# Reordering the start-up loads and PE's fillers, and splitting the last unit into half pairs, in a two-layer conditional convolution kernel

## What is computed

```python
# layer 0
x = x + conv1d(x, weight, groups=4, padding=4) + (cond @ c_weight.T)[:, :, None] + fside[None, :, None]
# layer 1
h = gelu(cond @ W0 + b0); h = gelu(h @ W1 + b1)
att = softmax(h @ W2 + b2)                      # (128, 8)
agg_w = einsum('bk,koi->boi', att, weight)      # one 64x64 matrix a sample
agg_b = att @ bias_k
x = x + einsum('boi,bih->boh', agg_w, x) + agg_b[:, :, None]
```

## Time and profile before

| | us |
|---|---|
| median of 3 runs (lowest, highest) | 248.84 (248.31, 249.13) |
| the profiled execution | 249.11 |
| its span in the trace | 247.3 |
| PE busy | 237.3 (96%) |
| DVE busy | 220.3 (89%) |
| ACT busy | 126.6 (51%) |
| POOL busy | 10.4 (4%) |

### The profile page before, as it was taken

The page is one execution under the profiler, slowest core; times in us unless marked ns, Lnnn a source line. Parts: engine busy times, 40 slices in busy tenths (PEclk is TensorE's granted clock), DMA queues, the critical chain, the costliest instruction groups (busy, mean ns, idle before and its releaser), DMA issues.

```text
span 247.3 us, 5763 instructions
## 1 busy us (share of the span) xinstructions
PE 237.3 (96%) x2162; PEld 103.9 (42%) x2162; DVE 220.3 (89%) x113; ACT 126.6 (51%) x208; POOL 10.4 (4%) x36
## 2 busy tenths in 40 slices
PE   6799999999999999999999999999999999999991
PEld 4643334344344444444444444444444444444530
DVE  1075899999999999999999999999999999999582
ACT  2457007374535456383645445373745446263772
POOL 1325000000000000000000000000000000000000
PEclk9689999999999999999999999999999999999999
DMA  7998566999999999999999999999999997444448
GB/s 189 307 326 240 152 125 191 258 312 365 357 322 268 359 263 383 249 380 238 334 294 292 327 256 378 247 388 239 362 273 322 298 281 293 170 170 172 171 184 328
DMA packets 28555, 68.39 MB, mean 277 GB/s; under 512 B 3184, under 2 KB 3568, under 8 KB 28544
## 3 DMA queue, kind: packets, MB, share of 16 engines
q1 hardware_dynamic: 19104, 50.98, 62.3%
q10 hardware_dynamic: 9440, 17.26, 26.5%
HBM read 34.67 MB, written 33.55 MB: 276 GB/s over the span
## 4 chain that ended last, share of the span: by engine, by line
PE 91%; DVE 3%; ACTq 2%; ACT 1%; issue 1%; DVEq 0%
PE yps L528 64%; PE zps L551 21%; PE yps L608 3%; DVE ynat L433 2%; ACTq L285 2%; PE yps L565 1%; PE zps L577 1%; DVE ycol L424 1%; PE yps L509 0%; PE yps L623 0%; PE yps L588 0%; ACT mixt L317 0%; DVE xin L498 0%; PE zps L588 0%; ACT L324 0%
## 5 line engine op out<-in xcount | busy, mean ns | idle before, releaser
L528 PE MATMUL yps<-xph,wraw 64*64 64x512 f32 x1512 | 169.0, 589 | 0.0
L303 ACT ACTIVATE zout<-zps,gamu 128x512 f32<-128x512 f32 x120 | 72.7, 688 | 95.3 <-PE zps L551 75.6
L528 PEld LDWEIGHTS yps<-xph,wraw 64*64 64x64 f32 x1512 | 67.5, 132 | 94.0 <-issue 94.0
L424 DVE STREAM_TRANSPOSE ycol<-yps 128x1024 f32<-128x1024 f32 x63 | 75.2, 1224 | 7.0 <-PE yps L528 5.4
L402 DVE STREAM_TRANSPOSE xph<-xin 128x4160 f32<-128x4160 f32 (+2 forms) x17 | 71.7, 4220 | 5.1 <-DMA xin<-in_x 5.1
L433 DVE STREAM_TRANSPOSE ynat<-ycol 128x4096 f32<-128x4096 f32 x15 | 66.7, 4446 | 1.1
L551 PE MATMUL zps<-ynat,mixv 64*64 64x512 f32 x480 | 57.8, 589 | 0.3 <-DVE ynat L433 0.3
L312 ACT ACTIVATE mixv<-mixt 64x256 f32 (+1 forms) x64 | 42.4, 663 | 1.4 <-ACT mixt L317 0.2
L551 PEld LDWEIGHTS zps<-ynat,mixv 64*64 64x64 f32 x480 | 21.6, 133 | 29.9 <-issue 29.6
L608 PE MATMUL yps<-zout 128*128 128x256 f32 x26 | 10.4, 566 | 1.3 <-POOL zout L243 1.3
L241 POOL COPY gamu<-gam 128x4 f32 (+1 forms) x16 | 2.9, 188 | 199.9 <-ACT zout L303 191.8
(11 more groups left out here) (56 smaller groups left out, 34.8 us busy)
## 6 DMA issues: line engine op xcount, KB each, us to landing
out<-zout SPq DMA_DIRECT2D x60, 512.0 KB, 6.2
xin<-in_x SPq DMA_DIRECT2D x64, 258.0 KB, 7.2
xin<-in_x ACTq DMA_DIRECT2D x64, 258.0 KB, 7.4
out<-xin SPq DMA_DIRECT2D x2, 512.0 KB, 2.7
out<-xin SPq DMA_DIRECT2D x4, 256.0 KB, 3.0
mlps<-in_mlp SPq DMA_DIRECT2D x1, 233.5 KB, 2.8
wraw<-in_conv_w ACTq DMA_DIRECT2D x1, 208.0 KB, 3.7
zout<-in_const_w SPq DMA_DIRECT2D x1, 160.0 KB, 9.3
```

Of the source, the lines that this page charges most:

```text
L303: nc.scalar.activation(zout[:, o].rearrange("p (i c j q) -> p c i j q", i=2, c=2, q=PH)[:, c], zps[:, at:at + BANK].rearrange("p (q i j) - ...
L424: nc.vector.transpose(ycol[:, :, :, :, :, g].rearrange("p i s j q c -> p (i s j) q c"), yps[:, 2 * BANK * (g % 2):2 * BANK * (g % 2) + 2 * ...
L528: last = nc.tensor.matmul(yps[C * c:C * c + C, at:at + BANK].rearrange("p (s f) -> p s f", s=S // 2), wsum[rows, b, g], xph[slot][rows, g, ...
```

## The change

At the start, ACT's first DMA is now `shares` (SP's no longer), then it waits for POOL's zero and runs the warming Gelu, and only then issues `mixw` and unit 0's x. `wraw` is issued after `h1`, ahead of unit 1's first pair of pieces; unit 1's second pair is issued after the Exp and `beta`. The copy of `wraw` to the lower partitions moves from DVE to ACT, behind `attt` and ahead of the gathers. On POOL, `const_eye` comes before `w_sum`. On PE a `keep_on(1)` is added behind L637 and behind L639; before `output_constants` PE now waits for `agg_out` 1 and runs `keep_on(2)`, and `keep_on(1)` stands behind it in place of 3.

In the last unit all four pairs are mixed, evacuated and stored in halves, in the order `LAST`: six halves on ACT, the last two on DVE, eight stores of 256 KB. `z_half` gives the place in PSUM of each half.

```diff
+LAST = (0, 0), (2, 0), (0, 1), (2, 1), (1, 0), (3, 0), (1, 1), (3, 1)
...
         def z_half(o, i):
+            bank, at = {(0, 0): (zps, 0), (2, 0): (yps, 2), (0, 1): (zps, 2), (2, 1): (zps, 0),
+                        (1, 0): (yps, 0), (3, 0): (yps, 2), (1, 1): (zps, 2), (3, 1): (zps, 0)}[o, i]
+            return bank[:, BANK * at:BANK * at + 2 * BANK].rearrange("p (c h f) -> p h c f", c=2, h=2)[:, 0]
...
             sp.dma_start(mlps[:], mlp).then_inc(mlp_in, 16)
-            sp.dma_start(shares[:], share).then_inc(share_in, 16)
             load(0, 0)
...
-            for o in (0, 2):
-                sp.wait_ge(z_act, o + 2)
-                sp.dma_start(z_rows(NU - 1, o), out_last(o)).then_inc(z_out[o], 16)
-            for o, i, made, n in ((1, 0, z_act, 5), (1, 1, z_dve, 1), (3, 0, z_act, 6), (3, 1, z_dve, 2)):
-                sp.wait_ge(made, n)
+            for n, (o, i) in enumerate(LAST):
+                sp.wait_ge(z_act if n < 6 else z_dve, n % 6 + 1)
                 sp.dma_start(z_rows(NU - 1, o)[:, H * i:H * i + H], out_half(o, i)).then_inc(z_out[o], 16)
...
-            act.dma_start(wraw[0:C], conv_w).then_inc(w_in, 16)
+            act.dma_start(shares[:], share).then_inc(share_in, 16)
+            act.wait_ge(zeroed, 1)
+            nc.scalar.activation(warm[:], warm[:], ACT.Gelu)
             act.dma_start(mixw, mix_w).then_inc(mix_in, 16)
             load(0, 0)
-            act.wait_ge(zeroed, 1)
-            nc.scalar.activation(warm[:], warm[:], ACT.Gelu)
-            load_block(1, 1, 0)
             act.wait_ge(mlp_in, 16)
             act.wait_ge(mm, 1)
             nc.scalar.activation(h1, sps[:, 0:NS], ACT.Gelu, bias=b0s).then_inc(act_mlp, 1)
-            load_block(1, 1, 1)
+            act.dma_start(wraw[0:C], conv_w).then_inc(w_in, 16)
+            load_block(1, 1, 0)
...
             nc.scalar.activation(beta[0:C], gps[0:C, 0:NS], ACT.Identity, bias=fsides[0:C]).then_inc(beta_made, 1)
+            load_block(1, 1, 1)
...
                 nc.scalar.activation(attt[:, o], sps[:, 0:NS], ACT.Copy, scale=turn[:, o:o + 1]).then_inc(soft, 1)
+            act.wait_ge(w_in, 16)
+            nc.scalar.activation(wraw[C:P], wraw[0:C], ACT.Copy).then_inc(w_both, 1)
             gather(0, 1, 4)
...
+            for n, (o, i) in enumerate(LAST[:6]):
+                act.wait_ge(last_mixes, n + 1)
+                evacuate_half(o, i)
...
-            dve.wait_ge(w_in, 16)
-            nc.vector.tensor_copy(wraw[C:P], wraw[0:C]).then_inc(w_both, 1)
...
             nc.tensor.matmul(gps[0:C, 0:NS], cws, condt, start=True, stop=True).then_inc(beta_mm, 1)
+            keep_on(1)
             pe.wait_ge(act_mlp, 1)
             nc.tensor.matmul(sps[:, NS:2 * NS], w1s, h1, start=True, stop=True).then_inc(mm, 1)
+            keep_on(1)
...
             aggregates()
+            pe.wait_ge(agg_out, 1)
+            keep_on(2)
             output_constants()
-            keep_on(3)
+            keep_on(1)
...
             pe.wait_ge(mixv_made, 4 * NU)
+            pe.wait_ge(last_nat, 1)
+            pe.wait_ge(z_made, 8 * NU - 10)
+            mix_half(0, 0)
+            pe.wait_ge(last_cols, 2)
+            mix_half(2, 0)
             pe.wait_ge(last_nat, 2)
-            pe.wait_ge(z_made, 8 * NU - 10)
-            mix_first(0)
             pe.wait_ge(z_made, 8 * NU - 8)
-            mix_first(2)
+            mix_half(0, 1)
+            pe.wait_ge(z_act, 1)
+            mix_half(2, 1)
             pe.wait_ge(last_nat, 3)
             pe.wait_ge(last_cols, 4)
             mix_half(1, 0)
+            pe.wait_ge(z_act, 2)
             mix_half(3, 0)
             pe.wait_ge(last_nat, 4)
-            pe.wait_ge(z_act, 2)
+            pe.wait_ge(z_act, 3)
             mix_half(1, 1)
             pe.wait_ge(z_act, 4)
             mix_half(3, 1)
```

More of the change, by code:

```diff
@@ L159, in y_last @@
                 "p (i h f) -> p h i f", i=2, h=2)[:, 0]
-        def z_first(o):
-            return zps[:, BANK * o:BANK * o + 2 * BANK].rearrange("p (c f) -> p c f", c=2)
         def z_half(o, i):
-            return (yps, zps)[i][:, BANK * (o - 1):BANK * (o - 1) + 2 * BANK].rearrange(
-                "p (c h f) -> p h c f", c=2, h=2)[:, 0]
+            bank, at = {(0, 0): (zps, 0), (2, 0): (yps, 2), (0, 1): (zps, 2), (2, 1): (zps, 0),
+                        (1, 0): (yps, 0), (3, 0): (yps, 2), (1, 1): (zps, 2), (3, 1): (zps, 0)}[o, i]
+            return bank[:, BANK * at:BANK * at + 2 * BANK].rearrange("p (c h f) -> p h c f", c=2, h=2)[:, 0]
         def out_last(o):
@@ L223, in _ @@
                     store(u, o)
-            for o in (0, 2):
-                sp.wait_ge(z_act, o + 2)
-                sp.dma_start(z_rows(NU - 1, o), out_last(o)).then_inc(z_out[o], 16)
-            for o, i, made, n in ((1, 0, z_act, 5), (1, 1, z_dve, 1), (3, 0, z_act, 6), (3, 1, z_dve, 2)):
-                sp.wait_ge(made, n)
+            for n, (o, i) in enumerate(LAST):
+                sp.wait_ge(z_act if n < 6 else z_dve, n % 6 + 1)
                 sp.dma_start(z_rows(NU - 1, o)[:, H * i:H * i + H], out_half(o, i)).then_inc(z_out[o], 16)
             for o in range(PR):
-                sp.wait_ge(z_out[o], 16 * NU + 16 * (o % 2))
+                sp.wait_ge(z_out[o], 16 * NU + 16)
         @block.gpsimd
@@ L254, in _ @@
                 nc.gpsimd.tensor_tensor(own, own, same.rearrange("p (h c) -> p h c", h=2), ALU.add).then_inc(mix_eye, 1)
-            pool.wait_ge(w_both, 1)
-            nc.gpsimd.tensor_tensor(wsum[:, 1], wsum[:, 1], wraw[:, NT * G:].broadcast_to([P, G, C]),
-                                    ALU.add).then_inc(w_sum, 1)
             pool.wait_ge(const_in, 16)
@@ L262, in _ @@
                                     ALU.add).then_inc(const_eye, 1)
+            pool.wait_ge(w_both, 1)
+            nc.gpsimd.tensor_tensor(wsum[:, 1], wsum[:, 1], wraw[:, NT * G:].broadcast_to([P, G, C]),
+                                    ALU.add).then_inc(w_sum, 1)
             pool.wait_ge(const_out, 1)
@@ L376, in _ @@
             act.wait_ge(turned, NU)
[L378 to L382, removed]
             def evacuate_half(o, i):
@@ L495, in _ @@
             dve.wait_ge(gam_cut, NU)
-            for n, o in enumerate((1, 3)):
-                dve.wait_ge(last_mixes, 5 + n)
+            for n, (o, i) in enumerate(LAST[6:]):
+                dve.wait_ge(last_mixes, 7 + n)
                 nc.vector.tensor_scalar(
-                    out_half(o, 1).rearrange("p (c j q) -> p c j q", c=2, q=PH),
-                    z_half(o, 1).rearrange("p c (q j) -> p c j q", q=PH),
+                    out_half(o, i).rearrange("p (c j q) -> p c j q", c=2, q=PH),
+                    z_half(o, i).rearrange("p c (q j) -> p c j q", q=PH),
                     gamu[1][:, o:o + 1], None, ALU.add).then_inc(z_dve, 1)
@@ L570, in conv_last @@
                 last.then_inc(last_conv, 1)
[L572 to L581, removed]
             def mix_half(o, i):
@@ L589, in mix_half @@
                             z_half(o, i)[C * s:C * s + C, c].rearrange("p (n j) -> p n j", j=NJ),
-                            mixv[1][rows, 2 * o + s], ynat[1][rows, o // 2, :, i, 2 + s],
+                            mixv[1][rows, 2 * o + s], ynat[1][rows, o // 2, :, i, 2 * (o % 2) + s],
                             start=True, stop=True)
```

## The result

| | before | after |
|---|---|---|
| median of 20 runs each | 248.72 us | 249.92 us |
| lowest run | 247.91 us | 248.60 us |
| ratio after/before (95% interval) | | 1.0065 (1.0047 to 1.0083) |
| span of the profiled execution | 247.3 us | 249.7 us |
| first convolution matmul starts | 19.4 us | 22.3 us |

The change makes the kernel 0.65% slower by the ratio (1.6 us); the two medians lie 1.2 us apart. The ratios leave out two executions that lie over 1.5% above the fastest of their kernel, one of 422.17 us before the change and one of 251.81 us (granted clock 0.982) of f4_old_loads_filled. Nothing moved in the steady part: two convolution blocks still take 5.16 us. The first mix came 3.4 us later and the tail became 1.0 us shorter, which is the 2.4 us between the two spans.

A forecast was written before the change was run, and what follows sets the result against it. PE alone was taken to bound the middle, leaving only the two ends; head 1.4 plus tail 0.8 made 2.2 us, so the median should be 246.6 us, range 245.9 to 248.4.

The forecast's parts named there:

- What bounds the kernel: Whole kernel: PE alone bounds 35.85 to 237.16 us; only the ends can move, the start by at most 1.9 us.
- Table first: Start, ACT: the earlier table load brings h1 forward 1.14 us, to 4.97, and h2 0.48 us, to 6.93.
- The clock early: Start, PE: if added fillers keep the upper clock from 4.7 us, the aggregates start at 11.6 and not 14.71.
- rival 1: Start, PE: the clock falls early as before; head gains 0.45 us, tail 0.8, total 247.6 us; chance 0.20.
- The loads: Start, DMA: 208 KB less ahead of unit 0's x land it at about 12.4 us; `wraw` lands near 13.6.
- rival 3: Start, DMA: `wraw` lands at 15 and not 13.6 us, the head gains nothing, total 248.0 us; chance 0.06.
- The copy on ACT, a new wait: Start, ACT: gathers queue behind the 0.85 us copy of `wraw`; with the clock kept, the gather runs 14.45 to 15.45.
- The clock late: Start, PE: idle from about 12.8 to 15.45 us, the clock may fall there and slow what follows.
- rival 2: Start, PE: clock falls late, head loses 1.5 us, total 249.5, chance 0.12; with early return 247.6, chance 0.08.
- The sum: Both ends: head 1.4 plus tail 0.8 gain 2.2 us, median 246.6 us; chance 0.44.
- Does it carry through: Start to first mix: DVE turns block 0 out by 22.9 us, so the mix moves as much as the first convolution.
- The tail: Last unit: half-pair stores close the 0.9 us DMA gap; gain 0.8 us, lower bound 0.3.

The follow-up runs named there:

- f4_old_loads_filled: Load order and DVE's copy as before; from the change the table load, unit 1's pairs, short fillers, tail; six fillers behind output constants: 247.67 us, ratio 0.9950.
- e1: The kernel before with only the new last unit by half pairs: 247.55 us, ratio 0.9948 against before.
- f1: The kernel after with ACT's copy of `wraw` moved behind the first two gathers: 248.05 us, ratio 0.9974 against before.
- f2: The kernel after with five filler matmuls between the two halves of the aggregates: 248.62 us, ratio 0.9988 against before.
- g1: As f1, with `keep_on(4)` in place of `keep_on(1)` behind the output constants: 247.94 us, ratio 0.9973 against before.
- g3: As g1, with `shares` issued by SP again and not by ACT: 248.07 us, ratio 0.9979 against before.
- e4: The kernel after with `wraw`'s load moved ahead of unit 0's x on ACT's queue: 249.72 us, ratio 1.0025 against before.
- f3: As e4, with six fillers and not one behind the output constants: 248.18 us, ratio 0.9975 against before.

## Why the prediction was wrong

- **What bounds the kernel.** Right that only the two ends can move. Incomplete in front: I read x of unit 0 at 13.03 us, unit 1 at 19.37, from one execution and took them as fixed. In the other four profiles with `wraw` ahead of x they are at 14.2 to 14.9 and 20.2 to 21.1. The 1.9 us "to be had" were then 0 to 0.7 us in those four: 14.57 + 4.51 us of transpose, for one, is 19.1, against 19.4. In such executions the network's chain and x's transpose arrive nearly together, and shortening one of them alone gives next to nothing (f4 against e1).
- **Table first.** h1 came at 5.62 us (4.97 forecast), mostly since the first fillers took 3.78 us and not 3.40 in this execution, h2 at 7.54 (6.93). Right in kind, 0.6 us off, and without weight.
- **The clock early.** Right: 1.00 from 5 to past 14 us, fillers at 0.24 to 0.26 us a record, aggregates at 12.37 and not 14.71 (11.6 forecast). So rival 1 didn't come.
- **The loads: the step that failed first.** `wraw` landed at 15.7, not 13.6: rival 3, and outside the bounds of 13.0 to 14.5. The step is "x lands at about 12.4", which took the 13.03 us of one execution and subtracted bytes over rate. x landed at 14.42, 2.0 us later than forecast, and with `wraw` behind it never before 13.2 (seven profiles). The next term, 1.2 us from x to `wraw`, was about right: 1.3 us here. That the 13.03 was an early landing could not be seen in a single trace. With the copy's 0.90 us (0.85 forecast) the first gather ran at 16.70 and not 14.45, 2.25 us later than forecast.
- **The copy on ACT, a new wait.** The mechanism was named, its place in the queue as well, and f1 confirms it: 2.3 us by the ratios for two lines in another order. The sum kept this wait at 14.45 us, where it cost nothing against before; what failed was its size.
- **The clock late: the second step that failed; it is rival 2 that happened.** The sum said of the way from the gather's end to the convolution that "it stays" 2.53 us, and so priced PE's new idle piece at nothing beyond its length. PE stood from 14.4 to 17.77 us, the clock fell, and from the gather's end to the convolution it took 4.6 us and not 2.53; with 0.40 us in the convolutions that is 2.5 us, against 2.9 forecast. I had given it 0.12, and 0.08 to its mild form. Of the 20 executions only two have a clock of 1.00, so it has to be near 0.9 (the list doesn't say where the clock fell). The sign of its condition was in my own sum, since an idle piece of 2.7 us was set beside a fall that had followed 0.49 us of work in 1.4.
- **The sum.** With `wraw` at 15.7 and the clock kept, the convolution would start at 17.73 + 2.53 = 20.3, 0.9 us later than before; less the tail's 1.0 that is 248.6, and the two executions with a clock of 1.00 are at 248.60 and 248.65. Where x and `wraw` landed in those two isn't recorded; f2 shows the case with its trace: ACT's copy at 15.60 us, the clock kept, the first convolution at 19.96, 248.62 us. The clock's fall brings the rest. The two rivals came together, and the second was made likely by the first; I had treated them as separate cases.
- **Does it carry through.** Wrong in a point that the other errors hid. Once the first convolution is early, DVE is behind unit 1's x, and the first mix follows that landing by 15.0 us (f1, g1, g3). In f1 DVE turned block 0 out by 24.11 us, not by 22.9.
- **The tail.** Right, and 0.2 us larger than taken: 1.0 us, the closed gap. The limit that I had set against it, 3.0 us from the last issue to its landing, was 2.8. The Trainium skill's advice to batch transfers to 1 MiB or more ("DMA: Bandwidth & Descriptors", section "Bandwidth") would have spoken for whole pairs. Here the measurement decides: the halves overlap in the queue, and the row of eight shows 2.8 us each.

The best versions are e1 (before, with the new tail) at a ratio of 0.9948 and f4 at 0.9950; they can't be told apart, and e1 is the smaller change. No head tried here was measurably better than the one of before. Left open: why x's landing wanders by 1 us and more between executions, and how much of it the order of `wraw` decides. With `wraw` behind x it is at 13.2 to 14.4 (seven profiles, mean 13.7), ahead of it, loaded once, at 13.0 to 14.9 (five, mean 14.3). The means differ by the 0.6 us that the forecast gave to the order, but by less than the spread within each.

## What to carry to other kernels

Before a load is moved behind others, ask which in-order queue waits for it and what stands behind that wait; here a 0.9 us copy ahead of the gathers held them for a DMA. Where several chains meet at one start, take the landing of a DMA from several executions, and count a shortened chain only up to the next one. An idle piece of PE that a change opens must be priced with the clock of what follows, not with its length alone, and the list of single executions with their clocks shows that executions differ; whether and where PE ran at the lower pace is seen in a trace, by the granted clock and by the length of the same instructions.

## What the runs showed of the hardware

- A fall of TensorE's granted clock follows a wait and is paid behind it: in e4 the wait of 3.2 us ends with 0.89 as the mean of its stretch, and the convolutions behind it run at 0.50. With a clock of 1.00 the same program (e4) took 247.9 us at the least, with 0.982 up to 251.1. That is the rule of the Trainium skill's "TensorE: Matmul & The Clock Gate", Part 1, which holds activity responsible for the upper level; the profiles of e4 and f3 agree.
- The recorded clock does not show every slow stretch: in e1's profile it reads 1.00 while six filler records take 2.86 us, as they did at 0.50 before; at the upper clock six take 1.30 us.
- A second load of `wraw` (208 KB, 64 rows of 3328 bytes) ahead of x cost far more than its bytes: it moved x's landing by 2.3 us (14.66 to 16.96), where bytes at 300 GB/s make 0.7. For the first load the means of the profiles give only 0.6 us. The cause of the difference isn't shown.
